# Values and gates of a gated linear attention computed in one 512-column product instead of two of 256 columns

## The reference

```python
x = x + 0.5 * ffn(layernorm(x)); x = x + attn(layernorm(x)); x = x + 0.5 * ffn(layernorm(x))

def attn(x):                       # 4 heads, keys of 128, values of 64
    q, k, v = heads(x @ Wq), heads(x @ Wk), heads(x @ Wv)        # Wv: 512 x 256
    gk = log_sigmoid(heads(x @ Wgk1 @ Wgk2 + bgk2)) / 16         # decay, from its logits
    o = chunked_linear_attention(q, k, v, gk)                    # chunks of 64 tokens
    g = x @ Wg                                                   # Wg: 512 x 256
    return (rms_norm(o) * Wnorm * (g * sigmoid(g))) @ Wo
```

## Time and profile before

| | |
|---|---|
| median of 3 runs | 1887.09 us (1886.38 to 1887.24) |
| the profiled execution | 1890.33 us, its span 1888.6 us |
| PE / PE weight loads busy | 1857.5 us (98%) / 1551.5 us (82%) |
| DVE, ACT, POOL busy | 801.9, 527.9, 128.2 us |
| granted TensorE clock, mean | 0.997 of 2.4 GHz |
| matmuls | 8896 |

### The profile page before, as it was taken

The page is one execution under the profiler, slowest core; times in us unless marked ns, Lnnn a source line. Parts: engine busy times, 40 slices in busy tenths (PEclk is TensorE's granted clock), DMA queues, the critical chain, the costliest instruction groups (busy, mean ns, idle before and its releaser), DMA issues.

```text
span 1888.6 us, 22836 instructions
## 1 busy us (share of the span) xinstructions
PE 1857.5 (98%) x8896; PEld 1551.5 (82%) x8896; DVE 801.9 (42%) x1478; ACT 527.9 (28%) x801; POOL 128.2 (7%) x224
## 2 busy tenths in 40 slices
PE   5999999999999999999999999999999999999998
PEld 4888888888888888888888888888888888888887
DVE  5555554545354544323334455354544324322222
ACT  3334422533124432112212533123432111311111
POOL 1121110000000100000010000000000000000000
PEclk9999999999999999999999999999999999999999
DMA  5877786445664456576576555564455566567664
GB/s 169 309 266 262 277 292 207 153 149 176 209 222 157 151 168 205 182 257 210 209 246 220 168 191 167 187 231 167 157 171 178 203 237 212 207 227 254 224 235 160
DMA packets 93131, 390.68 MB, mean 207 GB/s; under 512 B 11584, under 2 KB 11968, under 8 KB 70496
## 3 DMA queue, kind: packets, MB, share of 16 engines
q1 hardware_dynamic: 54096, 286.74, 43.1%
q10 hardware_dynamic: 27600, 47.15, 9.1%
q0 software_dynamic: 11328, 55.32, 7.4%
HBM read 347.36 MB, written 41.81 MB: 206 GB/s over the span
## 4 chain that ended last, share of the span: by engine, by line
PE 95%; DVE 3%; ACT 1%; issue 1%; DMA 1%; SPq 0%; POOL 0%; DVEq 0%; ACTq 0%
PE bank L975 27%; PE bank L977 27%; PE bank L976 27%; PE bank L1203 4%; PE bank L985 1%; PE bank L1146 1%; PE bank L1145 1%; PE bank L1138 1%; PE bank L1132 1%; PE bank L1190 0%; DVE act_t L620 0%; PE bank L1191 0%; PE bank L1005 0%; PE bank L1022 0%; PE bank L1006 0%
## 5 line engine op out<-in xcount | busy, mean ns | idle before, releaser
L975 PE MATMUL bank<-x_hi,wt 128*128 128x512 f32 x1408 | 557.1, 396 | 2.7 <-ACT sig L554 2.7
L977 PE MATMUL bank<-x_lo,wt 128*128 128x512 f32 x1408 | 549.7, 390 | 0.0
L976 PE MATMUL bank<-x_hi,wt 128*128 128x512 f32 x1408 | 549.3, 390 | 0.0
L620 DVE TENSOR_TENSOR act_t<-bank,sig 128x512 f32<-128x512 f32 x176 | 121.6, 691 | 565.7 <-PE bank L1203 556.0
L977 PEld LDWEIGHTS bank<-x_lo,wt 128*128 128x128 f32 x1408 | 264.6, 188 | 56.9
L975 PEld LDWEIGHTS bank<-x_hi,wt 128*128 128x128 f32 x1408 | 265.0, 188 | 55.0 <-issue 2.9
L976 PEld LDWEIGHTS bank<-x_hi,wt 128*128 128x128 f32 x1408 | 265.1, 188 | 52.3
L975 PE MATMUL bank<-dt,a_hi 128*128 128x512 f32 x704 | 279.2, 397 | 0.3 <-DVE a_lo L620 0.3
L977 PE MATMUL bank<-dt,a_hi 128*128 128x512 f32 x704 | 275.1, 391 | 0.0
L976 PE MATMUL bank<-dt,a_lo 128*128 128x512 f32 x704 | 274.2, 389 | 0.0
L554 ACT ACTIVATE sig<-bank 128x512 f32<-128x512 f32 x176 | 105.4, 599 | 484.2 <-PE bank L1203 484.1
(11 more groups left out here) (168 smaller groups left out, 1709.6 us busy)
## 6 DMA issues: line engine op xcount, KB each, us to landing
wt<-scr_w SPq DMA_DIRECT2D x154, 1152.0 KB, 5.2
dt<-scr_d SPq DMA_DIRECT2D x154, 512.0 KB, 5.1
s_bc<-scr_s ACTq DMA_DIRECT2D x128, 256.0 KB, 5.3
scr_w<-wt POOLq DMA_DIRECT2D x22, 1152.0 KB, 6.5
state<-wat POOLq DMA_DIRECT2D x28, 512.0 KB, 5.4
b_all<-wgu SPq DMA_DIRECT2D x22, 512.0 KB, 5.5
scr_d<-dt POOLq DMA_DIRECT2D x22, 512.0 KB, 5.4
s_bc<-scr_s ACTq DMA_DIRECT2D x32, 192.0 KB, 4.7
```

The costliest lines, as they stand in the source:

```text
L620: return nc.vector.tensor_tensor(dst, a, b, op)
L975: mm(dst, wh, xh, start=start, stop=False)
L976: mm(dst, wl, xh, start=False, stop=False)
L977: return mm(dst, wh, xl, start=False, stop=stop)
```

## The change

The values' and the gates' weights lie side by side: the first two slabs now hold, for two of the four 128-row parts of the model dimension each, 512 columns (256 of values, 256 of gates). Slots 13 to 16 compute one tile of 128 tokens each, 12 matmuls of 512 columns into W0. DVE copies the values half into `vtz`, then ACT takes the Silu of the gates half, and the next of these slots waits for that. Slots 20 and 21 have no work left on PE. Since W0 is taken, the decay logits of all four heads go to W1, and each waits for the absolute values of the head before it. The first slab of queries and keys can be split only after slot 16 (both halves of `tw` are in use until then): its split goes from slot 16 to 18, that of the second from 22 to 20.

```diff
-        SPLIT = {4: S_V, 9: S_G, 16: S_QK, 22: S_QK + 1, 24: S_QK + 2, 26: S_QK + 3, 28: S_WO}
+        SPLIT = {4: S_VG, 9: S_VG + 1, 18: S_QK, 20: S_QK + 1, 24: S_QK + 2, 26: S_QK + 3, 28: S_WO}
...
-                pool.wait_ge(gt_ok, 2 * t + 2)
+                pool.wait_ge(gt_ok, (t + 1) * NT)
...
-                elif s == S_QK + 1:
-                    act.wait_ge(g_mm, 2 * t + 2)
-                elif s == S_QK:
-                    act.wait_ge(v_mm, 2 * t + 2)
+                elif s >= S_QK:
+                    act.wait_ge(vg_mm, (t + 1) * NT)
...
+                if k in (13, 14, 15, 16):
+                    i = k - 13
+                    act.wait_ge(vt_ok, t * NT + i + 1)
+                    if i == 0:
+                        wait(act, og_ok, t * H)
+                    nc.scalar.activation(gt[:, i, :], W0[:, 2 * P:4 * P], ACT.Silu).then_inc(gt_ok, 1)
...
-                    nc.scalar.activation(spl[:, h, :], (W1, W0)[h % 2][:], ACT.Abs, bias=bias[:, h:h + 1]).then_inc(zabs_ok, 1)
+                    nc.scalar.activation(spl[:, h, :], W1[:], ACT.Abs, bias=bias[:, h:h + 1]).then_inc(zabs_ok, 1)
...
-                elif k in (20, 21):
-                    i = k - 20
-                    act.wait_ge(g_mm, 2 * t + i + 1)
...
-                elif k in (13, 15):
-                    i = (k - 13) // 2
-                    dve.wait_ge(v_mm, 2 * t + i + 1)
+                if k in (13, 14, 15, 16):
+                    i = k - 13
+                    dve.wait_ge(vg_mm, t * NT + i + 1)
...
-                    nc.vector.tensor_copy(z[0:CK, :, 0, :], v[0:CK, :, :])
-                    nc.vector.tensor_copy(z[CK:P, :, 1, :], v[CK:P, :, :]).then_inc(vt_ok, 1)
+                    v = W0[:, 0:2 * P].rearrange("p (h v) -> p h v", v=DV)
+                    nc.vector.tensor_copy(vtz[0:CK, i, :, 0, :], v[0:CK, :, :])
+                    nc.vector.tensor_copy(vtz[CK:P, i, :, 1, :], v[CK:P, :, :]).then_inc(vt_ok, 1)
...
+                if k in (13, 14, 15, 16):
+                    i = k - 13
+                    if i == 0:
+                        pe.wait_ge(x_lo_ok, r * NT + 3)
                     else:
                         pe.wait_ge(x_lo_ok, r * NT + 4)
-                        pe.wait_ge(vt_ok, 2 * t + 1)
...
+                        pe.wait_ge(gt_ok, t * NT + i)
+                    for kk in range(KC):
+                        hi, lo = slab(S_VG + kk // 2)
+                        ins = three(W0[:], xk(s, kk, cols(i)), (hi[:, kk % 2, :], lo[:, kk % 2, :]), kk == 0, kk == KC - 1)
+                    ins.then_inc(vg_mm, 1)
...
-                    elif h == 1:
-                        pe.wait_ge(vt_ok, 2 * t + 2)
                     else:
-                        pe.wait_ge(zabs_ok, t * H + h - 1)
-                    mm((W1, W0)[h % 2][:], gk2_s[:, cols(h)], zs[:], start=True, stop=True).then_inc(z_mm, 1)
-                elif k in (20, 21):
...
+                        pe.wait_ge(zabs_ok, t * H + h)
+                    mm(W1[:], gk2_s[:, cols(h)], zs[:], start=True, stop=True).then_inc(z_mm, 1)
...
-                    if h == 0:
-                        pe.wait_ge(gt_ok, 2 * t + 1 + is_k)
+                    if h == 0 and is_k:
+                        pe.wait_ge(gt_ok, (t + 1) * NT)
+                    elif h == 0:
+                        pe.wait_ge(zabs_ok, (t + 1) * H)
```

More of the change, by code:

```diff
@@ L41 @@
 SLABS = 7
-S_V, S_G, S_QK, S_WO = 0, 1, 2, 6
+S_VG, S_QK, S_WO = 0, 2, 6
 PHASES = 8
@@ L178, in build @@
         dve_step = sem("dve_step")
-        v_mm, g_mm, vt_ok, gt_ok, gtw_ok, z1_ok, zs_hi_ok, zs_ok, z_mm, zmin_ok, zabs_ok, zexp_ok, zln_ok = (
-            sem(n) for n in ("v_mm", "g_mm", "vt_ok", "gt_ok", "gtw_ok", "z1_ok", "zs_hi_ok", "zs_ok", "z_mm", "zmin_ok",
+        vg_mm, vt_ok, gt_ok, gtw_ok, z1_ok, zs_hi_ok, zs_ok, z_mm, zmin_ok, zabs_ok, zexp_ok, zln_ok = (
+            sem(n) for n in ("vg_mm", "vt_ok", "gt_ok", "gtw_ok", "z1_ok", "zs_hi_ok", "zs_ok", "z_mm", "zmin_ok",
                              "zabs_ok", "zexp_ok", "zln_ok"))
@@ L313, in attention @@
                     pool.wait_ge(o_ok, t * H)
-                load_t(t, S_V)
+                load_t(t, S_VG)
                 rstd_of(LN_T[t])
-                for n in range(S_G, S_QK + 2):
+                for n in range(S_VG + 1, S_QK + 2):
                     load_t(t, n)
-                pool.wait_ge(gt_ok, 2 * t + 2)
+                pool.wait_ge(gt_ok, (t + 1) * NT)
                 if t == 0:
@@ L393, in t_hi @@
                     act.wait_ge(k_mm, t * H + s - S_QK - 1)
[L394 to L398 removed]
+                elif s >= S_QK:
+                    act.wait_ge(vg_mm, (t + 1) * NT)
+                elif s == S_VG:
                     wait(act, k_mm, t * H)
@@ L471, in attention @@
                     hi(r, i, s, (W0, W1)[i % 2])
-                elif k == 14:
+                if k == 14:
                     act.wait_ge(z1_ok, t + 1)
@@ L827, in attention @@
                         dve.wait_ge(routeT_ok, 3 * (q + 1))
-                    nc.vector.tensor_scalar(zmin[:, h, :], (W1, W0)[h % 2][:], bias[:, h:h + 1], 0.0, ALU.add,
+                    nc.vector.tensor_scalar(zmin[:, h, :], W1[:], bias[:, h:h + 1], 0.0, ALU.add,
                                             ALU.min).then_inc(zmin_ok, 1)
@@ L1041, in attention, with slab @@
                 r, s = LN_T[t], (q + 1) % 2
-                def slab(n):
-                    n += t * SLABS
+                def slab(s):
+                    n = t * SLABS + s
                     pe.wait_ge(t_lo_ok, n + 1)
-                    w = tw[:, n % 2, :].rearrange("p (a k c) -> p a k c", a=2, k=KC)
+                    w = tw[:, n % 2, :].rearrange("p (a k c) -> p a k c", a=2, k=2 if s < S_QK else KC)
                     return w[:, 0, :, :], w[:, 1, :, :]
@@ L1087, in attention @@
                         pe.wait_ge(zs_ok, t + 1)
-                    elif h == 1:
-                        pe.wait_ge(vt_ok, 2 * t + 2)
-                    else:
-                        pe.wait_ge(zabs_ok, t * H + h - 1)
-                    mm((W1, W0)[h % 2][:], gk2_s[:, cols(h)], zs[:], start=True, stop=True).then_inc(z_mm, 1)
-                elif k in (20, 21):
[L1094 to L1101, removed]
+                    else:
+                        pe.wait_ge(zabs_ok, t * H + h)
+                    mm(W1[:], gk2_s[:, cols(h)], zs[:], start=True, stop=True).then_inc(z_mm, 1)
                 elif 22 <= k <= 29:
@@ L1135, in attention @@
                         pe.wait_ge(sc_cp, t * H + h + 1)
-                        pe.wait_ge(vt_ok, 2 * t + 2)
+                        pe.wait_ge(vt_ok, (t + 1) * NT)
                         for i in range(NT):
@@ L1284 @@
     heads = [np.concatenate([fold(f[n][:, h * P:(h + 1) * P]) for n in ("attn_Wq", "attn_Wk")], axis=-1) for h in range(H)]
-    wat = np.stack([w.reshape(P, GW) for w in (fold(f["attn_Wv"]), fold(f["attn_Wg"]), *heads, fold(f["attn_Wo"]))])
+    values_gates = np.concatenate([fold(f["attn_Wv"]), fold(f["attn_Wg"])], axis=-1)
+    wat = np.stack([w.reshape(P, GW) for w in (values_gates[:, 0:2], values_gates[:, 2:4], *heads, fold(f["attn_Wo"]))])
     inv = f["ffn_inv_map"]
```

7 lines of the change are left out of this document (1 added, 6 removed).

## The result

The changed kernel took 1890.62 us (median of 22 runs) against 1887.14 us (22 runs) of the kernel before: ratio 1.0017, 95% interval 1.0012 to 1.0023, which is 3.2 us slower (2.3 to 4.3). (The ratio goes by the means of the runs; the two medians lie 3.5 us apart.) The forecast was 1889.6 us, 2.5 us slower. The profiled execution has a span of 1891.1 us, 2.5 more than before.

What follows compares the result with a forecast made beforehand. The prediction took PE's own instruction stream as the bound. The joined product's -2.9 us and the fourth logit's +5.4 us give +2.5 us on 1887.09, so 1889.6 us, with a range of 1886.6 to 1891.8 us.

Steps and rivals of the forecast that it cites:

- PE is the bound, and a wait put in is paid in full: Slots 13 to 21: PE is busy throughout, so removed work is gained and added waits are paid in full.
- The joined product, 0.18 us per slot: Slots 13 to 16: half the matmuls save 0.15 us, the group after them 0.03; four attentions, -2.9 us.
- The first copies, 0.42 us: Slot 17: DVE's 64 x 256 copies, taken as 0.42 us, leave the second logit unwaiting with 0.27 us to spare.
- The rival of the late head 1: Slot 17: dearer copies cost PE 0.25 us more per attention, 1890.6 us; chance 0.07.
- The fourth logit, 1.34 us: Slot 19: PE waits behind slot 18's split and the third head's absolute values, 1.34 us per attention, +5.4 in all.
- the covered wait: Rival for slot 19: the fourth logit's wait is covered, only the saving is left, 1884.2 us; chance 0.08.
- the falling clock: Rival for slot 19: PE's clock falls during the wait, 1.7 us four times, 1896.4 us; chance 0.03.
- the dear columns: Rival for slots 13 to 16: joined matmuls are not cheaper per column, wait stays, 1892.5 us; chance 0.03.
- It keeps 1.9 us to spare: At `down(6)`: `a_lo` ends 14.3 us after the third logit, PE arrives at 16.2, so no wait.
- the forecast's own formula: PE's loss at a wait: end of the releasing instruction + 0.38 us - (PE's arrival + 0.23 us).
- the sentence that POOL's multiplication moves ahead of a load that is not due: On POOL: the gates' weighting moves ahead of the third slab's load, not due before slot 24; counted as nothing.
- The total: Whole kernel: -2.9 + 5.4 = +2.5 us, 1889.6 us, 0.13% slower; terms' bounds +1.2 to +4.0.

Runs made afterwards that it cites:

- Experiment 2: The changed kernel with the first query and key slab's split in slot 19, its low part behind the fourth head's minimum on DVE; ratio 0.9989 to the kernel before.
- experiment 3: The changed kernel with each 512-column matmul of slots 13 to 16 taken apart into two of 256 columns; ratio 1.0040 to the kernel before.
- experiment 1: The changed kernel with the split of the first query and key slab in slot 19 instead of 18; ratio 1.0008 to the kernel before.
- experiment 5: The changed kernel with the slab's low part in slot 18 moved behind the third logit's minimum on DVE; ratio 1.0025 to the kernel before.
- experiment 4: The kernel before with all four heads' logits in W1, values and gates still apart, gates' banks swapped; ratio 1.0032 to the kernel before.
- experiment 6: As experiment 5, with POOL's multiplication of the gates ahead of the load of the second query and key slab; ratio 0.9988 to the kernel before.

## Why the prediction was right

- *PE is the bound, and a wait put in is paid in full*: right. Slots 13 to 22 grew by 0.65 us in the first attention and by 0.63 in each of the others; forecast 0.62.
- *The joined product, 0.18 us per slot*: right. Experiment 2 has 0.72 us per attention without any wait, as forecast; experiment 3 gives 0.64 back.
- *The first copies, 0.42 us*: they took 0.41 and 0.43, and the second logit didn't wait. The rival of the late head 1 is out.
- *The fourth logit, 1.34 us*: it was 1.37, through the links named. Experiments 1, 2 and 5 take the wait away with the split's place, experiment 4 brings it to another logit. The rivals of the covered wait, the falling clock (1.00 in the slots) and the dear columns (experiment 3) are out.
- *"It keeps 1.9 us to spare"*, for `down(6)`: wrong. The fourth head's absolute values started 7.54 us after the third logit, not 5.85, since DVE stood still behind POOL's multiplication, and `a_lo` ended at 16.0, not 14.3. PE came to `down(6)` at 16.22, so by the forecast's own formula (end + 0.38 against arrival + 0.23) 0.07 us were left. The step that failed is the sentence that POOL's multiplication moves ahead of a load that is not due: I costed the queue on POOL, and not what its instruction does to DVE. It cost nothing in the changed kernel only because PE was late itself, which is luck. Experiments 5 and 6 show its price, 1.33 us per attention, once the first wait is gone.
- *The total*: +2.5 forecast, +3.2 measured; the interval, 2.3 to 4.3, holds the forecast, and PE's own stream has +2.8. The agreement of the two spans (2.5) is partly luck: -1.12, +2.91 and -2.09 us of stretches that scatter nearly cancel in it.

## What to carry to other kernels

When a buffer is taken from a chain, find for each of its users how much work covers one round, and then look at what else stands in the queues between the links: the same chain was in time at two heads and 1.4 us late at the third, where a 1.2 us split stood in the way. On a kernel that one engine bounds, the order on the helper engines costs nothing as long as the bound engine doesn't wait for it. So move the long piece behind the short one that the bound engine waits for, and check the wait behind it before counting the gain: experiment 5 took away 1.4 us and got 1.3 back eleven microseconds later.

## What the runs showed of the hardware

- A DVE instruction that reads two operands in SBUF was held while POOL's tensor multiplication ran: 2.49, 2.65 and 1.26 us instead of 0.69, ending 0.56, 0.56 and 0.55 us after POOL's end, which is 0.13 less than its own length. It is so in all four attentions of every kernel in which the two meet. The instruction before it, with one operand in PSUM, overlapped the multiplication at 0.68 and 0.69 us. The Trainium skill (SBUF — State Buffer, section Who interferes with whom) says that the two engines share a port pair, which such a DVE instruction and a GpSimd instruction that reads SBUF take one after the other; the traces agree.
- PE that had waited for another engine paid a little beyond the wait: the matmul behind the first came 0.34 us after it at the logits and 0.30 us at `down(6)` (experiments 1 and 5), not 0.23.
- Three places scatter between executions of otherwise equal work: the start up to slot 13 of the first attention (297.9 to 298.5 us in eight of the twelve profiled kernels, 299.6 to 300.6 in four), the 512 KB behind four stores (the split starts 6.8 to 10.3 us after the load's issue in the eight kernels that have it so), and the end after the last matmul start (5.8 us twice, 3.7 ten times). The start goes with the granted clock of phase 0: in the four it was 1.00 from 38 to 46 us and 0.50 to 0.53 from 48 to 50, after PE had idled 2.7 us before 41 to 42 us and 2.1 to 2.2 us before 46 to 48; in the eight it was 0.50 from 38 to 44 us and 1.00 from 48 on. Each of the three is about as large as the effect studied here. That is why the stretches of the traces decide these experiments, and the totals of experiments 1 and 5, each over 2 us above its expectation, are left unexplained.
